# Context and key operands laid in longer rows, key blocks cut at 320 and 296 columns

## Chip, cores and metric

The kernel runs on one NeuronCore of a Trainium2 chip (trn2). The metric is the device time of one execution in microseconds, lower is better; the time of a kernel is the median of its runs.

## What is computed

Four cross-attention layers follow each other on a stream `x` of shape (8, 512, 512). All four attend to the same context `ctx` of shape (8, 77, 1024). Layers 0 and 2 are of one kind ("A"), layers 1 and 3 of another ("B"). Cut to what matters:

```python
def kind_A(x, ctx, mask_A, mask_B, Wq, Wk, Wv, Wo, bo, tok_A, tok_B):   # 16 heads of 64
    q, k, v = heads(x @ Wq), heads(ctx @ Wk), heads(ctx @ Wv)
    logits = einsum('bhqd,bhkd->bhqk', q, k) * 64 ** -0.5
    bias = zeros((512, 77))
    bias[:, tok_A] = -20 * (1 - mask_A)[:, None]
    bias[:, tok_B] = -20 * (1 - mask_B)[:, None]
    out = einsum('bhqk,bhkd->bhqd', softmax(logits + bias), v)
    return merge(out) @ Wo + bo + x

def kind_B(x, ctx, wq, wk, wv, wo, norm_w):                             # 16 heads of 32, 4 key heads
    q = heads(rmsnorm(x, norm_w) @ wq)
    k, v = heads(ctx @ wk), heads(ctx @ wv)
    out = softmax_over_context(q, k, v, scale=32 ** -0.5)
    return x + merge(out) @ wo
```

Everything is float32.

## The kernel before

Every product of two float32 matrices is made of three TensorE passes: an operand is split in a part rounded to `fp32r` ("hi") and the rest ("lo"), and the passes are hi x hi, hi x lo and lo x hi (`three_passes`, L259 to L263, or the same three written out). Each pass is one MATMUL with a weight load of its own (the stationary operand, up to 128 columns), then up to 512 columns of the moving operand stream past it.

**The context part** (`context_part`, L290 to L597) comes first. `ctx_s` holds the transposed context, hi and lo: for each of 8 chunks `k` of 128 channels a row of 616 values (8 batches x 77 tokens). For each of nine blocks of 256 weight columns (`j`), TensorE makes

- the keys: for two groups `m` of 128 columns and two halves `h` of the 616 context columns (`n = 2m + h`), 8 chunks x 3 passes with the weights stationary and `ctx_s` **moving**, 308 columns each: `keys` at L558, 9 x 4 x 8 x 3 = 864 matmuls;
- the values: for five groups `r` of 128 context columns (the last has 104) 8 chunks x 3 passes with `ctx_s` **stationary** and 256 weight columns moving: `values` at L567, 9 x 5 x 8 x 3 = 1080 matmuls.

ScalarE rounds each result out of its bank (L415, L422), VectorE subtracts for the rest (L464, L470), and the SP queue stores both in DRAM (`k_scr`, `v_scr`). `k_out`, the tile that the keys are stored from, has rows of 616 values.

**The main part** (`whole_block`) walks over 128 units (four layers x eight batches x four groups of heads; unit `u` uses slot `u % 2`). For each unit the SP queue loads keys into `keys_s[:, slot]` (L699), block-diagonal, so that one matmul serves several heads; TensorE makes the scores of four tiles of 128 tokens. For kind A a tile takes 2 x 3 matmuls of 154 columns (`keys[:, c, h]`, L807, L810, L813: `c` is a pair of heads, `h` hi or lo), for kind B it takes 3 matmuls of 308 columns (L824, which is L261 to L263). So 1536 short ones of kind A and 768 of kind B have `keys_s` as moving operand. The short ones are issued one by one between matmuls of 512 columns of the query projection (L847 to L851) or of the values (L889): `beside`, L942, with two of 512 columns after each short one in tiles 0 and 1 of a steady unit. VectorE takes the maximum and subtracts (L1165, L1169), ScalarE exponentiates, POOL multiplies by the reciprocal sums (L1326), TensorE transposes (L869), multiplies by the values (L889), and projects (L261 to L263 on `acc_bank`). The order on each engine is written out by hand in step loops; four groups of PSUM banks with two banks each pass the work on.

**Where the operands lie.** The tensors are placed one behind the other in each partition. In the kernel before, `w_s`, `x_s`, `o_s`, `q_s`, `ctx_s` and `keys_s` begin on a multiple of 128 bytes and the rows of the first four are 2048 bytes or more. A row of `ctx_s` is 616 x 4 = 2464 bytes, which is 19 x 128 + 32, and the second half of a row begins 1232 bytes in, which is 9 x 128 + 80. So the moving operand of the keys begins 0, 32, 64, 96, 0, 32, 64, 96 bytes past a multiple of 128 for `k` = 0 to 7 in the first half and 80, 112, 16, 48, 80, 112, 16, 48 in the second; hi and lo alike. In `keys_s` a slot has 2464 bytes and a kind A block 616: the short operands `(c, h)` = (0,0), (0,1), (1,0), (1,1) begin 0, 104, 80, 56 bytes past a multiple of 128 in slot 0, and 32, 8, 112, 88 in slot 1. Those of kind B, `h` = 0 and 1, begin 0 and 80 past it in slot 0, 32 and 112 in slot 1. `x_front`, `mx`, `sums`, `rinv` and `ms` begin 64 past one. The context part's tensors are given back at once (`early.close()`, L347), so the main part's lie over them: `o_s` to `unused` over `ctx_s`, `q_s` over `kvw_raw`, `prob` over `k_out`, `pT_s` over `v_out`.

Of the kernel before, what the change touches and what calls it, by code (L numbers as in the profile page):

```python
# [36 lines left out]
SC = GH * CTX  # L37
PART = 2048
BLK = 256
HALF = ROWS // 2  # L40
SUPPRESS, EPS = 20.0, 1e-5
VROWS = [min(P, ROWS - P * r) for r in range(-(-ROWS // P))]

# [246 lines left out]
def context_part(nc, ctx, lasting, ctxT, kvw, k_scr, v_scr, k1_scr, v1_scr, x_in, wqA, boA, normB, masks, tokens,  # L290
# [7 lines left out]
    def sb(name, shape, dt):  # L298
        return early.enter_context(nc.sbuf_tensor(name, shape, dt))
# [2 lines left out]
        return ctx.enter_context(nc.semaphore(name))  # L302

    ctx_raw = sb("ctx_raw", [P, KC, ROWS], F32)
    ctx_s = sb("ctx_s", [P, 2, KC, ROWS], F32R)
    w_raw = sb("kvw_raw", [P, 2, PART], F32)
    k_out = sb("k_out", [P, 2, 2, ROWS], F32R)
    v_out = sb("v_out", [P, len(VROWS), 2, BLK], F32R)
# [89 lines left out]
    def scalar(act):  # L398
        def split_weights(slot, j):
            if j:  # L400
                act.wait_ge(w_loaded[slot], 16 * (j + slot))
                if slot == 0:
                    act.wait_ge(k_mm, 4 * j)
                else:
                    act.wait_ge(v_mm, NV * j)
            else:
                act.wait_ge(w_loaded[slot], 16)
            act.activation(w_s[:, slot, 0], w_raw[:, slot], ACT.Copy).then_inc(w_hi[slot], 1)

        def drain_keys(n, j):  # L410
            m, h = n // 2, n % 2
            act.wait_ge(k_mm, 4 * j + n + 1)
            if n == 0 and j:
                act.wait_ge(k_stored, keys_stored(j))
            act.activation(k_out[:, m, 0, h * HALF:(h + 1) * HALF], banks[n][:, 0:HALF], ACT.Copy)\  # L415
               .then_inc(k_hi, 1)

        def drain_values(r, j):
            act.wait_ge(v_mm, NV * j + r + 1)
            if r == 0 and j:  # L420
                act.wait_ge(v_stored, vals_stored(j))
            act.activation(v_out[0:VROWS[r], r, 0], banks[4 + r % 4][0:VROWS[r], 0:BLK], ACT.Copy)\  # L422
               .then_inc(v_hi, 1)

        def split_late(n):

            act.wait_ge(late_loaded[n], 16)
            act.activation(late_parts(n)[0], w_raw[:, n % 2], ACT.Copy).then_inc(late_hi, 1)

        for k in range(KC):  # L430
            if k % 2 == 0:
                act.wait_ge(first_loaded[k // 2], 16)
                act.activation(w_s[:, 0, 0, BLK * k:BLK * (k + 2)], w_raw[:, 0, BLK * k:BLK * (k + 2)], ACT.Copy).then_inc(first_hi, 1)
            if k == 0:
                act.wait_ge(chunk_loaded, 16)
            else:
                act.wait_ge(ctx_loaded[k // 2], 16)
            act.activation(ctx_s[:, 0, k], ctx_raw[:, k], ACT.Copy).then_inc(ctx_hi, 1)
        split_weights(1, 0)
        for j in range(NJ):  # L440
            for n in range(4):
                drain_keys(n, j)
            if j + 1 < NJ:
                split_weights(0, j + 1)
            else:
                split_late(1)
                split_late(2)
            for r in range(NV):
                drain_values(r, j)
            if j + 1 < NJ:  # L450
                split_weights(1, j + 1)
            if j + 2 == NJ:
                split_late(0)

    def vector(dve):
# [5 lines left out]
        def drain_keys(n, j):  # L461
            m, h = n // 2, n % 2
            dve.wait_ge(k_hi, 4 * j + n + 1)
            dve.tensor_tensor(k_out[:, m, 1, h * HALF:(h + 1) * HALF], banks[n][:, 0:HALF],  # L464
                              k_out[:, m, 0, h * HALF:(h + 1) * HALF].bitcast(F32), ALU.subtract)\
               .then_inc(k_lo, 1)

        def drain_values(r, j):
# [9 lines left out]
        for k in range(KC):  # L478
            if k % 2 == 0:
                dve.wait_ge(first_hi, k // 2 + 1)  # L480
                dve.tensor_tensor(w_s[:, 0, 1, BLK * k:BLK * (k + 2)], w_raw[:, 0, BLK * k:BLK * (k + 2)],
                                  w_s[:, 0, 0, BLK * k:BLK * (k + 2)].bitcast(F32), ALU.subtract).then_inc(first_lo, 1)
            dve.wait_ge(ctx_hi, k + 1)
            dve.tensor_tensor(ctx_s[:, 1, k], ctx_raw[:, k], ctx_s[:, 0, k].bitcast(F32), ALU.subtract)\
               .then_inc(ctx_lo, 1)
        split_weights(1, 0)
        links = [0]
# [69 lines left out]
    def tensor(pe):  # L557
        def keys(n, k):  # L558
            m, h = n // 2, n % 2
            mm = three_passes(pe, banks[n][:, 0:HALF],  # L560
                              [w_s[:, 0, s, BLK * k + m * P:BLK * k + m * P + P] for s in range(2)],
                              [ctx_s[:, s, k, h * HALF:(h + 1) * HALF] for s in range(2)],
                              k == 0, k == KC - 1)
            if k == KC - 1:
                mm.then_inc(k_mm, 1)

        def values(r, j):  # L567
            if NV * j + r >= 4:
                pe.wait_ge(v_lo, NV * j + (1 if r == 4 else 0))
            for k in range(KC):  # L570
                mm = three_passes(pe, banks[4 + r % 4][0:VROWS[r], 0:BLK],
                                  [ctx_s[:, s, k, r * P:r * P + VROWS[r]] for s in range(2)],
                                  [w_s[:, 1, s, BLK * k:BLK * (k + 1)] for s in range(2)],
                                  k == 0, k == KC - 1)
            mm.then_inc(v_mm, 1)

        for k in range(KC):
            if k % 2 == 0:
                pe.wait_ge(first_lo, k // 2 + 1)
            pe.wait_ge(ctx_lo, k + 1)  # L580
            for n in range(4):
                keys(n, k)
        for j in range(NJ):
            if j:
                pe.wait_ge(w_lo[0], j)
                pe.wait_ge(k_lo, 4 * j)
                for n in range(4):
                    for k in range(KC):
                        keys(n, k)
            pe.wait_ge(w_lo[1], j + 1)  # L590
            for r in range(NV):
                values(r, j)
# [7 lines left out]
def whole_block(nc, lasting, context_args, x_in, stream, k_scr, v_scr, k1_scr, v1_scr, wqA, woA, wqB, woB):  # L600

    with ExitStack() as ctx:
# [7 lines left out]


        vals_s = sb("vals_s", [P, 2, 4, 2, P], F32R)
        keys_s = sb("keys_s", [P, 2, 2 * SC], F32R)
        x_front = sb("x_front", [P, RING, TOK], F32)
        mx = sb("mx", [P, 2, 4 * GH], F32)
        sums = sb("sums", [P, 2, 4 * GH], F32)
        rinv = sb("rinv", [P, 2, 4 * GH], F32)
        ms = sb("ms", [P, 2, TILES], F32)
        rstd = sb("rstd", [P, 2, TILES], F32)

        o_s = sb("o_s", [P, 2, 8, TOK], F32R)
        xsq = sb("xsq", [P, TOK], F32)
        x_power = sb("x_power", [P, TOK], F32)
        rest = sb("rest", [P, TILES, P], F32)
        sb("unused", [P, 128], F32)

        q_s = sb("q_s", [P, 2, 2, 2, TOK], F32R)
        prob = sb("prob", [P, 2, TILES, SC], F32)
# [166 lines left out]
        def _(pe):  # L795
            def scores(u, t):
                slot, out, tok = u % 2, s_bank[t % 2], slice(t * P, t * P + P)
                if kind(u).name == "A":
                    pe.wait_ge(s_biased, plan.biased(u, t))
                    keys = keys_s[:, slot].rearrange("q (c h n) -> q c h n", c=2, h=2)  # L800
                    for c in range(2):
                        if t == 0:
                            pe.wait_ge(q_out, plan.q[("q", u, c)] + 1)
                            if c == 0:
                                pe.wait_ge(keys_loaded[slot], plan.keys_count(u))
                        cols = out[:, 2 * CTX * c:2 * CTX * (c + 1)]
                        pe.matmul(cols, q_s[:, slot, 0, c, tok], keys[:, c, 0], start=False, stop=False,  # L807
                                  skip_group_check=True)
                        yield
                        pe.matmul(cols, q_s[:, slot, 0, c, tok], keys[:, c, 1], start=False, stop=False,  # L810
                                  skip_group_check=True)
                        yield
                        mm = pe.matmul(cols, q_s[:, slot, 1, c, tok], keys[:, c, 0], start=False, stop=c == 1,  # L813
                                       skip_group_check=True)
                        if c == 1:
                            mm.then_inc(s_mm, 1)
                        yield
                else:
                    pe.wait_ge(s_sub, TILES * u + t - 1)
                    if t == 0:  # L820
                        pe.wait_ge(q_out, plan.q[("q", u, 0)] + 1)
                        pe.wait_ge(keys_loaded[slot], plan.keys_count(u))
                    keys = keys_s[:, slot].rearrange("q (h n) -> q h n", h=2)
                    three_passes(pe, out[:, 0:SC], [q_s[:, slot, h, 0, tok] for h in range(2)],  # L824
                                 [keys[:, h] for h in range(2)], True, True).then_inc(s_mm, 1)
                    yield
# [635 lines left out]
```

## Time and profile before

| | us |
|---|---|
| time of the kernel before, median of 3 runs | 2069.18 (2068.88 to 2070.52) |
| the profiled execution | 2069.05 |
| its span, first to last instruction | 2067.3 |
| PE (matmuls) busy | 2027.7, 98% of the span, 11482 matmuls |
| PEld (weight loads) busy | 1762.3, 85% |
| VectorE busy | 1404.0, 68% |
| ScalarE busy | 966.7, 47% |
| POOL busy | 646.3, 31% |

The profile is of one execution. Matmuls are pipelined and their ends are modelled, so that busy time on PE says little of how many more could be done; how long a matmul holds the engine is read from the starts: the distance from one start to the next in a stretch where nothing is waited for. The granted TensorE clock is shown in tenths of full speed (2.4 GHz).

### The profile page before, as it was taken

The numbers are of one execution on the slowest core, as the hardware profiler recorded it, in microseconds if no ns is written. First come the engines' busy times: TensorE is split into PE (matmuls) and PEld (weight loads), VectorE is DVE, ScalarE is ACT, GpSimd is POOL, SyncE is SP. The second block draws the span as 40 slices with busy tenths as digits, with TensorE's granted clock in tenths as the row PEclk, the third lists the DMA queues.
The fourth block names the chain that finished last, engine by engine and source line by source line (L and its number), as shares of the span: only waits on it lengthen the run. The fifth ranks groups of instructions, "written<-read, shape, count | busy, mean of one in ns | idle before, by whom it ended". The sixth has DMA issues, their size and how long they took to land.

```text
span 2067.3 us, 31200 instructions
## 1 busy us (share of the span) xinstructions
PE 2027.7 (98%) x11482; PEld 1762.3 (85%) x11482; DVE 1404.0 (68%) x2424; ACT 966.7 (47%) x1814; POOL 646.3 (31%) x518
## 2 busy tenths in 40 slices
PE   8999999999999998999999999999999989999998
PEld 8999988888888887788888888888888877888887
DVE  4432365775568556788888676557755675888886
ACT  3222263553445344555555454335433553555553
POOL 0000042322232254454443441223212533444441
PEclk9999999999999999999999999999999999999999
DMA  8688832222122222233333332212221232233322
GB/s 232 165 172 195 187 94 62 73 67 74 54 73 70 66 83 71 83 106 97 88 97 95 104 98 64 76 56 68 65 79 51 72 90 68 74 91 92 88 72 84
DMA packets 262537, 191.02 MB, mean 92 GB/s; under 512 B 197522, under 2 KB 199986, under 8 KB 259826
## 3 DMA queue, kind: packets, MB, share of 16 engines
q1 hardware_dynamic: 262386, 189.03, 34.8%
q8 instruction: 92, 1.51, 0.3%
q14 instruction: 59, 0.48, 0.1%
HBM read 132.66 MB, written 56.26 MB: 91 GB/s over the span
## 4 chain that ended last, share of the span: by engine, by line
PE 50%; issue 30%; POOL 11%; DVE 6%; ACT 1%; DMA 1%; SPq 0%; POOLq 0%; DVEq 0%; ACTq 0%
PE acc_bank L889 6%; POOL prob L1326 6%; PE t_bank L869 4%; PE acc_bank L261 4%; PE acc_bank L263 4%; PE acc_bank L262 4%; PE ctx_bank L261 4%; PE ctx_bank L262 4%; PE ctx_bank L263 4%; PE q_bank L847 4%; PE q_bank L849 3%; PE q_bank L851 3%; POOL x_s L1301 3%; PE s_bank L261 2%; POOL rest L1335 2%
## 5 line engine op out<-in xcount | busy, mean ns | idle before, releaser
L1326 POOL TENSOR_TENSOR prob<-prob,rinv 128x1232 f32<-128x1232 f32 x128 | 288.3, 2253 | 1011.4 <-DVE rinv L1207 1011.4
L1065 ACT ACTIVATE q_s<-q_bank 128x512 fp32r<-128x512 f32 x192 | 114.7, 597 | 491.6 <-PE q_bank L851 488.5
L889 PE MATMUL acc_bank<-pT_s,vals_s 128*128 128x512 f32 x1024 | 339.4, 417 | 0.0
L847 PE MATMUL q_bank<-x_s,w_s 128*128 128x512 f32 x768 | 319.9, 417 | 0.0
L849 PE MATMUL q_bank<-x_s,w_s 128*128 128x512 f32 x768 | 313.6, 408 | 0.0
L851 PE MATMUL q_bank<-x_s,w_s 128*128 128x512 f32 x768 | 313.0, 408 | 0.0
L1165 DVE TENSOR_REDUCE mx<-s_bank 128x4 f32<-128x308 f32 x512 | 239.9, 469 | 106.5 <-PE s_bank L813 54.1
L261 PE MATMUL acc_bank<-o_s,w_s 128*128 128x512 f32 x752 | 300.3, 399 | 0.2
L263 PE MATMUL acc_bank<-o_s,w_s 128*128 128x512 f32 x752 | 293.5, 390 | 0.0
L262 PE MATMUL acc_bank<-o_s,w_s 128*128 128x512 f32 x752 | 292.9, 390 | 0.0
L1056 ACT ACTIVATE prob<-prob,rstd 128x308 f32<-128x308 f32 x256 | 141.5, 553 | 265.5 <-DVE prob L1169 255.1
L1169 DVE TENSOR_TENSOR prob<-s_bank,mx 128x308 f32<-128x308 f32 x512 | 244.9, 478 | 26.4
L1192 DVE TENSOR_TENSOR pT_s<-t_bank,pT_s 128x512 fp32r<-128x512 f32 x256 | 175.6, 686 | 79.0 <-ACT pT_s L1079 79.0
L889 PEld LDWEIGHTS acc_bank<-pT_s,vals_s 128*128 128x128 f32 x1024 | 191.8, 190 | 28.3
L1224 DVE SCALAR_TENSOR_TENSOR x_back<-acc_bank,bo,x_back 128x512 f32<-128x512 f32 x64 | 47.8, 747 | 244.9 <-PE acc_bank L263 244.9
L1079 ACT ACTIVATE pT_s<-t_bank 128x512 fp32r<-128x512 f32 (+1 forms) x320 | 183.1, 589 | 35.0 <-PE t_bank L869 34.6
L869 PE MATMUL t_bank<-ident,prob 128*128 128x128 f32 (+1 forms) x1280 | 185.8, 274 | 1.1 <-DVE pT_s L1192 1.1
L1204 DVE TENSOR_REDUCE sums<-prob 128x16 f32<-128x1232 f32 x128 | 182.5, 1426 | 0.0
L869 PEld LDWEIGHTS t_bank<-ident,prob 128*128 128x128 f32 (+1 forms) x1280 | 155.7, 136 | 28.6 <-DVE pT_s L1192 1.6
L263 PEld LDWEIGHTS acc_bank<-o_s,w_s 128*128 128x128 f32 x752 | 141.1, 188 | 30.6
L261 PEld LDWEIGHTS acc_bank<-o_s,w_s 128*128 128x128 f32 x752 | 141.3, 188 | 28.7 <-DVE o_s L1198 1.8
L851 PEld LDWEIGHTS q_bank<-x_s,w_s 128*128 128x128 f32 x768 | 145.6, 190 | 23.2
(107 smaller groups left out, 4095.0 us busy)
## 6 DMA issues: line engine op xcount, KB each, us to landing
stream<-x_back SPq DMA_DIRECT2D x128, 256.0 KB, 2.6
x_front<-stream SPq DMA_DIRECT2D x96, 256.0 KB, 3.3
x_back<-stream SPq DMA_DIRECT2D x96, 256.0 KB, 3.9
kvw_raw<-kvw SPq DMA_DIRECT2D x17, 1024.0 KB, 8.4
k_scr<-k_out SPq DMA_DIRECT2D x36, 308.0 KB, 8.8
keys_s<-k_scr SPq DMA_DIRECT2D x128, 77.0 KB, 2.5
v_scr<-v_out SPq DMA_DIRECT2D x8, 1024.0 KB
vals_s<-v_scr SPq DMA_DIRECT2D x512, 6.5 KB
```

The costliest lines, as they stand in the source:

```text
L261: pe.matmul(out, weights[0], moving[0], start=start, stop=False)
L262: pe.matmul(out, weights[0], moving[1], start=False, stop=False)
L263: return pe.matmul(out, weights[1], moving[0], start=False, stop=stop)
L847: pe.matmul(out, w[0], x_now[0], start=k == 0, stop=False)
L849: pe.matmul(out, w[0], x_now[1], start=False, stop=False)
L851: mm = pe.matmul(out, w[1], x_now[0], start=False, stop=k == XC - 1)
L869: mm = pe.transpose(t_bank[(3 * u + n) % 2][0:rows, t * P:t * P + P], p, ident[:, :])
L889: mm = pe.matmul(out, w, pT_s[:, part], start=i == mine[0] and part == 2 * n and w is v[0], stop=i == mine[-1] and w is terms[-1][0] and p ...
L1079: act.activation(pT_s[0:rows, 2 * n], t_bank[(3 * u + n) % 2][0:rows, :], ACT.Copy).then_inc(t_hi, 1)
L1165: dve.tensor_reduce(top, scored, AX_X, ALU.max).then_inc(s_max, 1)
L1169: dve.tensor_tensor(prob[:, slot, t].rearrange("q (h n) -> q h n", h=GH), scored, top.unsqueeze(2).broadcast_to([P, GH, CTX]), ALU.subtrac ...
L1326: pool.tensor_tensor(view, view, rinv[:, slot].unsqueeze(2).broadcast_to([P, TILES * GH, CTX]), ALU.mult).then_inc(p_norm, 1)
```

## The change

`ctx_s` gets rows of 640 values (2560 bytes, 20 x 128) of which 616 are used, and the halves of the keys are 320 and 296 columns, so that the second begins 1280 bytes in. In `keys_s` a kind A block gets 160 values (640 bytes) of which 154 are used, a kind B block 320 (1280 bytes) of which 308 are used; a slot is 2560 bytes. So all moving and stationary operands in these two tensors begin on multiples of 128 bytes. `ms` and `rstd` move behind `rest`, and `unused` grows from 128 to 336 values. With that `x_front`, `mx`, `sums`, `rinv` and `ms` begin on multiples of 128 bytes too, `o_s`, `xsq`, `x_power` and `rest` lie 128 bytes higher, and `q_s`, `prob`, `pT_s`, `x_back` and `stage` 1024 bytes higher. `q_s` then begins 512 bytes below `kvw_raw` instead of on it.

The number and order of the instructions on each engine, the SP queue's among them, and what each waits for stay as they were. Forms change: the 864 key matmuls of 308 columns become 432 of 320 and 432 of 296, the 36 pairs of drains (L415, L464) likewise 18 of 320 and 18 of 296, and eight clears of `keys_s` on POOL take 640 instead of 616 values. Rows in DRAM, in `k_out` and in `prob` keep their lengths.

```diff
-HALF = ROWS // 2
+HALF = 320
+HALVES = [slice(0, HALF), slice(HALF, ROWS)]
+ROWS_LAID, SC_LAID, PAIR_LAID = 640, 320, 160
...
-    ctx_s = sb("ctx_s", [P, 2, KC, ROWS], F32R)
+    ctx_s = sb("ctx_s", [P, 2, KC, ROWS_LAID], F32R)
...
-            act.activation(k_out[:, m, 0, h * HALF:(h + 1) * HALF], banks[n][:, 0:HALF], ACT.Copy)\
+            cols = HALVES[h]
+            act.activation(k_out[:, m, 0, cols], banks[n][:, 0:cols.stop - cols.start], ACT.Copy)\
...
-            act.activation(ctx_s[:, 0, k], ctx_raw[:, k], ACT.Copy).then_inc(ctx_hi, 1)
+            act.activation(ctx_s[:, 0, k, 0:ROWS], ctx_raw[:, k], ACT.Copy).then_inc(ctx_hi, 1)
...
             m, h = n // 2, n % 2
-            mm = three_passes(pe, banks[n][:, 0:HALF],
+            cols = HALVES[h]
+            mm = three_passes(pe, banks[n][:, 0:cols.stop - cols.start],
                               [w_s[:, 0, s, BLK * k + m * P:BLK * k + m * P + P] for s in range(2)],
-                              [ctx_s[:, s, k, h * HALF:(h + 1) * HALF] for s in range(2)],
+                              [ctx_s[:, s, k, cols] for s in range(2)],
...
-        keys_s = sb("keys_s", [P, 2, 2 * SC], F32R)
+        keys_s = sb("keys_s", [P, 2, 2 * SC_LAID], F32R)
...
-        ms = sb("ms", [P, 2, TILES], F32)
-        rstd = sb("rstd", [P, 2, TILES], F32)
...
-        sb("unused", [P, 128], F32)
+        ms = sb("ms", [P, 2, TILES], F32)
+        rstd = sb("rstd", [P, 2, TILES], F32)
+        sb("unused", [P, 336], F32)
...
-                    keys = keys_s[:, slot].rearrange("q (c h n) -> q c h n", c=2, h=2)
+                    keys = keys_s[:, slot].rearrange("q (c h n) -> q c h n", c=2, h=2)[:, :, :, 0:PAIR]
...
-                    keys = keys_s[:, slot].rearrange("q (h n) -> q h n", h=2)
+                    keys = keys_s[:, slot].rearrange("q (h n) -> q h n", h=2)[:, :, 0:SC]
```

## Rows read from the trace of the kernel before

**Rows 1.** Page: span, busy time of each engine, granted clock in 40 slices.

```profile
span 2067.3 us, 31200 instructions
...
PE 2027.7 (98%) x11482; PEld 1762.3 (85%) x11482; DVE 1404.0 (68%) x2424; ACT 966.7 (47%) x1814; POOL 646.3 (31%) x518
...
PEclk9999999999999999999999999999999999999999
```

**Rows 2.** Groups by line and form (xcount, busy us, mean ns, idle before).

```profile
L813 PE MATMUL s_bank<-keys_s,q_s 128*128 128x154 f32 x512 | 119.5, 233 | 0.0
...
L263 PE MATMUL ctx_bank<-ctx_s,w_s 128*128 128x308 f32 x288 | 88.2, 306 | 0.0
...
L263 PE MATMUL s_bank<-keys_s,q_s 128*128 128x308 f32 x256 | 78.4, 306 | 0.0
...
L263 PE MATMUL ctx_bank<-w_s,ctx_s 128*128 128x256 f32 x288 | 80.8, 280 | 0.0
...
L263 PE MATMUL ctx_bank<-w_s,ctx_s 128*104 128x256 f32 x72 | 20.2, 281 | 0.0
...
L464 DVE TENSOR_TENSOR k_out<-ctx_bank,k_out 128x308 fp32r<-128x308 f32 x36 | 16.7, 476 | 55.7 <-ACT k_out L415 55.7
...
L1364 POOL MEMSET keys_s<- 128x616 f32 x6 | 3.7, 614 | 34.9 <-PE s_bank L813 29.4 <-PE s_bank L263 5.5
```

**Rows 3.** Timeline of PE, a block of context keys (start us, us, engine, line).

```profile
92.20 0.30 PE L261 MATMUL ctx_bank<-ctx_s,w_s 128*128 128x308 f32 x1
...
92.63 0.30 PE L261 MATMUL ctx_bank<-ctx_s,w_s 128*128 128x308 f32 x1
...
94.77 0.30 PE L261 MATMUL ctx_bank<-ctx_s,w_s 128*128 128x308 f32 x1
...
95.18 0.31 PE L261 MATMUL ctx_bank<-ctx_s,w_s 128*128 128x308 f32 x1
...
95.61 0.30 PE L261 MATMUL ctx_bank<-ctx_s,w_s 128*128 128x308 f32 x1
...
99.01 0.31 PE L261 MATMUL ctx_bank<-ctx_s,w_s 128*128 128x308 f32 x1
```

**Rows 4.** Timeline of PE, a projection of 512 columns.

```profile
670.15 0.39 PE L261 MATMUL acc_bank<-o_s,w_s 128*128 128x512 f32 x1
...
672.87 0.39 PE L261 MATMUL acc_bank<-o_s,w_s 128*128 128x512 f32 x1
```

**Rows 5.** Timeline of PE, first values block after those keys.

```profile
105.81 0.28 PE L261 MATMUL ctx_bank<-w_s,ctx_s 128*128 128x256 f32 x1
...
106.17 0.28 PE L261 MATMUL ctx_bank<-w_s,ctx_s 128*128 128x256 f32 x1
...
108.65 0.28 PE L261 MATMUL ctx_bank<-w_s,ctx_s 128*128 128x256 f32 x1
```

**Rows 6.** Timeline of PE, score tiles of units 28 and 29, kind A.

```profile
716.11 0.23 PE L807 MATMUL s_bank<-keys_s,q_s 128*128 128x154 f32 x1
...
717.83 0.23 PE L807 MATMUL s_bank<-keys_s,q_s 128*128 128x154 f32 x1
...
719.57 0.23 PE L807 MATMUL s_bank<-keys_s,q_s 128*128 128x154 f32 x1
...
727.52 0.23 PE L807 MATMUL s_bank<-keys_s,q_s 128*128 128x154 f32 x1
...
729.23 0.23 PE L807 MATMUL s_bank<-keys_s,q_s 128*128 128x154 f32 x1
...
730.94 0.23 PE L807 MATMUL s_bank<-keys_s,q_s 128*128 128x154 f32 x1
```

**Rows 7.** Timeline of PE, transposes, four to a row.

```profile
1015.14 0.60 PE L869 MATMUL t_bank<-ident,prob 128*128 128x128 f32 x4
1015.58 0.60 PE L935 MATMUL q_bank<-ident,x_power 128*128 128x128 f32 x4
```

**Rows 8.** List of waits, a PE row: who waited for whom, total us, times, longest.

```profile
PE s_bank L261 <- DVE prob L1169: 21.9, 24, 3.7
```

More of the change, by code:

```diff
@@ L463, in drain_keys @@
             dve.wait_ge(k_hi, 4 * j + n + 1)
-            dve.tensor_tensor(k_out[:, m, 1, h * HALF:(h + 1) * HALF], banks[n][:, 0:HALF],
-                              k_out[:, m, 0, h * HALF:(h + 1) * HALF].bitcast(F32), ALU.subtract)\
+            cols = HALVES[h]
+            dve.tensor_tensor(k_out[:, m, 1, cols], banks[n][:, 0:cols.stop - cols.start],
+                              k_out[:, m, 0, cols].bitcast(F32), ALU.subtract)\
                .then_inc(k_lo, 1)
@@ L483, in vector @@
             dve.wait_ge(ctx_hi, k + 1)
-            dve.tensor_tensor(ctx_s[:, 1, k], ctx_raw[:, k], ctx_s[:, 0, k].bitcast(F32), ALU.subtract)\
+            dve.tensor_tensor(ctx_s[:, 1, k, 0:ROWS], ctx_raw[:, k], ctx_s[:, 0, k, 0:ROWS].bitcast(F32), ALU.subtract)\
                .then_inc(ctx_lo, 1)
@@ L559, in keys @@
             m, h = n // 2, n % 2
-            mm = three_passes(pe, banks[n][:, 0:HALF],
+            cols = HALVES[h]
+            mm = three_passes(pe, banks[n][:, 0:cols.stop - cols.start],
                               [w_s[:, 0, s, BLK * k + m * P:BLK * k + m * P + P] for s in range(2)],
-                              [ctx_s[:, s, k, h * HALF:(h + 1) * HALF] for s in range(2)],
+                              [ctx_s[:, s, k, cols] for s in range(2)],
                               k == 0, k == KC - 1)
```

## Prediction, made before the changed kernel was run

> **What bounds the kernel.** I read the page first: PE is busy for 2027.7 of 2067.3 us at a granted clock of nine tenths or more in all 40 slices, while VectorE has 68%, ScalarE 47% and POOL 31% [rows 1]. So the time is the sum over TensorE's matmuls of how long each holds the engine, plus some waits, of which the largest that PE itself shows in the scores is 21.9 us in 24 places behind VectorE's subtraction [rows 8]. The change can move the time only by what a matmul costs. I therefore went to the groups by form for the counts, and then to the timeline of PE for distances between starts, because the mean ns of a group has a modelled end in it. At 2.4 GHz a column takes 1/2.4 = 0.4167 ns; what a start-to-start distance has above that I call the excess.
>
> - Keys of the context, 308 moving columns: 48 matmuls from 92.20 to 99.01 us, 6.81 / 48 = 141.9 ns; streaming is 308 / 2.4 = 128.3 ns, excess 13.6 ns [rows 3].
> - A projection, 512 moving columns: 12 matmuls from 670.15 to 672.87, 2.72 / 12 = 226.7 ns; streaming 213.3, excess 13.4 ns [rows 4].
> - Values of the context, 256 moving columns: 24 matmuls from 105.81 to 108.65, 118.3 ns; streaming 106.7, excess 11.6 ns [rows 5].
>
> This is the heart of the matter: the projection's operands (`o_s` and `w_s`) begin on multiples of 128 bytes in the kernel before, those of the keys for the most part do not, and the excess is the same within 0.2 ns. If a start off such a multiple cost anything, the keys would have to show it.
>
> **The change, part by part.** Counts: 864 key matmuls (3 x 288), 1080 value matmuls (3 x 288 + 3 x 72), 768 scores of kind B (3 x 256), 1536 of kind A (3 x 512) [rows 2]; 4248 of 11482 in all. Some begin on a multiple of 128 bytes already: two of the 16 chunks of the keys (108 matmuls), and of kind B's those in slot 0 with `h` = 0 (two passes of three of 384, so 256). That leaves 864 - 108 + 768 - 256 = 1268 of 308 columns that change.
>
> *The split 320/296.* The columns are the same in number. Between 308 and 512 columns the distance grows by (226.7 - 141.9) / 204 = 0.416 ns a column [rows 3, 4], so 320 costs about 5.0 ns more (146.9) and 296 5.0 ns less (136.9): 432 x 5.0 - 432 x 5.0 = 0. Bounds: the line through 256 and 512 columns, (226.7 - 118.3) / 256 = 0.423 a column, puts 308 at 140.3, so 141.9 could hold 1.6 ns of some rounding that 320 and 296 would lose: 864 x 1.6 = 1.4 us of gain; or they could keep it and each pay as much again: +1.4 us. I take 0, since the straight line is what the nearest rows give.
>
> *Alignment of the moving operand, keys.* The block is a trial by itself, because the eight chunks start at all offsets. One chunk is three matmuls. Chunk 0 (offset 0, aligned) takes 92.63 - 92.20 = 0.43 us; chunk 6 (offset 64) takes 95.18 - 94.77 = 0.41 us; the eight of the first half take 3.41 / 8 = 0.426, and the eight of the second half, none aligned, 3.40 / 8 = 0.425 [rows 3]. The aligned one is no cheaper. Upper end: all become like chunk 0, (0.430 - 0.4256) / 3 = +1.5 ns, x 864 = +1.3 us. Lower end: all become like the cheapest chunk, (0.410 - 0.4256) / 3 = -5.2 ns, x 864 = -4.5 us. I take 0: the cheapest is an unaligned one, and its rows are rounded to 0.01 us.
>
> *Scores of kind B.* The same form and width, and the same mean, 306 ns, as the keys [rows 2]; so the same price: 0, between 768 x 1.5 = +1.2 and 768 x -5.2 = -4.0 us.
>
> *Scores of kind A.* A pair `c` of a steady tile is three short matmuls and six of 512. In unit 28 (slot 0) the pair c = 0 takes 717.83 - 716.11 = 1.72 us, c = 1 takes 719.57 - 717.83 = 1.74; in unit 29 (slot 1) both take 1.71 [rows 6]. Slot 1 has no operand on a multiple of 128 and is the quickest. Six long ones are 6 x 0.2267 = 1.36 us, so a short one holds the engine for (1.71 - 1.36) / 3 = 117 ns to 127 ns though its 154 columns stream in 64 ns. Next to it stands the transpose: 128 columns (53 ns), yet one every (1015.58 - 1015.14) / 4 = 110 ns [rows 7]. Both are paced by the 128-column weight load, which hides any saving in the streaming. I take 0. Lower end: the 384 short ones of slot 0, c = 1 fall by the (1.74 - 1.71) / 3 = 10 ns to the others' level, -3.8 us; upper end: slot 1 rises to slot 0's c = 0, 768 x 3.3 ns = +2.5 us.
>
> *Stationary operand, values.* The first chunk (offset 0) takes 0.36 us, the next seven (108.65 - 106.17) / 7 = 0.354 [rows 5]. Aligned is not cheaper. All like the first: (0.36 - 0.355) / 3 = +1.7 ns, x 1080 = +1.8 us; below, the same distance, -1.8 us. I take 0.
>
> *The rest.* The drain of 308 columns takes VectorE 476 ns [rows 2]; in proportion 320 and 296 are 19 ns more and less, under a PE that waits for neither. POOL's clear of `keys_s` at 614 ns grows by at most 24/616 of that, 24 ns in each of eight, on an engine that is idle for 69% of the span. Its cover is large: a step of the main part is many us long. The move of `x_front` and of the small tiles concerns ScalarE, VectorE and POOL, which have 32 to 69% to spare. DMA issues keep number, size and order; no wait is added. Taken at nothing.
>
> **Sum.** 0 + 0 + 0 + 0 + 0 = 0 against the profiled execution's own 2069.05 us (span 2067.3 and 1.75 around it); the median of the runs is 2069.18, 0.13 above, and I predict **2069.2 us**. With every upper end at once it would be +1.4 + 1.3 + 1.2 + 2.5 + 1.8 = +8.2 us, with every lower end -1.4 - 4.5 - 4.0 - 3.8 - 1.8 = -15.5 us. The ends are independent and those below rest on the cheapest single readings, so the likeliest case has as its own range within 0.2% (4.1 us, about what a measurement of this kernel can tell from no change): 2065.1 to 2073.3.
>
> The Trainium skill (TensorE: Matmul & The Clock Gate, "Back-to-back issue gap") gives the gap of an isolated matmul as N / 2.4 + 2.5 ns, which would be 130.8 for 308 columns where the trace has 141.9. If aligned starts brought those 1268 matmuls down to it, that would be 11.1 ns x 1268 = 14.1 us of gain, an estimate of 2055 us. The trace speaks against it: the aligned 512 columns would be 215.8 ns by the page and take 226.7 [rows 4].
>
> **Rivals.**
>
> 1. *Off-multiple starts are the excess* (faster). 13.3 ns is just what 32 columns cost (32 / 2.4), and 32 columns are 128 bytes: each start between two multiples could cost one more piece of that size. Then the 1268 matmuls save 13.3 ns each, 16.9 us, and the result is 2052.3; the short ones stay at the weight load's pace. For it: the size of the excess. Against it: the aligned projection has the same excess, and chunk 0 takes no less than its neighbours [rows 3, 4]. Chance 0.05.
> 2. *A smaller saving of the same sort* (faster). The lower ends are partly real: steps of a chunk do differ by up to 0.02 us [rows 3]. If aligned operands all come out as the cheapest ones, 2069.2 - 15.5 = 2053.7; about half of it is 2061. Against it: in no stretch is the cheapest the aligned one. Chance 0.08.
> 3. *Aligned streams meet* (slower). The weight load of the next matmul and the moving operand of this one are read at the same time. With both on multiples of 128 they would begin in the same place each time and could hold each other up. Place: the 1268 matmuls of 308 columns. Price: chunk 0 is 0.43 where the mean is 0.4256; with the rounding of the rows against me it is 0.44, (0.44 - 0.4256) / 3 = 4.8 ns, x 1268 = 6.1 us, so 2075.3. It decides from 4.1 us / 1268 = 3.2 ns each. For it: the first chunk of keys and of values is each time the dearer [rows 3, 5]. Against it: the all-aligned projection has no more excess than the rest. Chance 0.07.
> 4. *The change does not do what it says*: streaming could be charged by whole pieces of 32 columns, so that 308, 320 and 296 all cost the same; or the transposes, whose `prob` rows of 1232 bytes stay unaligned, could be what matters. Either gives no difference in time and counts with the forecast.
>
> **How the numbers follow.** Within 0.2%: 0.80. Faster: 0.05 + 0.08 = 0.13. Slower: 0.07. For the range I take the 0.80 and reach a little into rivals 2 and 3, to 2062 (some 7 us of the 15.5) and 2075; outside lie rival 1, the larger half of rival 2 and the tail of rival 3, some 0.13.
>
> **What would show it.** Right: in the keys block pairs of halves still take 6.8 us for 48 matmuls, with 0.441 us for a chunk of 320 and 0.411 for one of 296; a kind A pair stays at 1.71 to 1.74 us; the transposes stay at 110 ns; PE stays busy for 98%. Wrong toward faster: 48 key matmuls in 6.2 us, or kind A pairs below 1.70. Wrong toward slower: the chunk of 320 above 0.45, or the eight value chunks of a group above 2.88 us. The forecast as a whole is wrong if the time leaves 2065.1 to 2073.3.

## The result, and the profile after

The changed kernel takes 2081.76 us (median of 4 runs, 2081.33 to 2082.30) against 2069.35 us before (4 runs, 2068.88 to 2070.52). The ratio is 1.0059, with a 95% interval from 1.0046 to 1.0073: it is slower by 12.4 us, where no change had been forecast and the range ended at 2075. The profiled execution took 2082.3 us with a span of 2080.5, so 13.2 us more than the span before.

The page first, the lines that answer to [rows 1]:

```profile
span 2080.5 us, 31200 instructions
...
PE 2039.4 (98%) x11482; PEld 1762.5 (85%) x11482; DVE 1404.3 (67%) x2424; ACT 966.7 (46%) x1814; POOL 645.3 (31%) x518
...
PEclk9999999999999999999999999999999999999999
```

The other engines are busy within 1 us of what they were; PE is busy for 11.7 us more at the same number of matmuls, and the granted clock stays at nine tenths or more in every slice. So the time is in what matmuls cost, as the prediction had it, and the question is which. The groups by line and form (count, busy us, mean ns, idle before) answer; the changed kernel's lines have numbers two to five higher, so that `three_passes` is L263 to L265:

```profile
L263 PE MATMUL acc_bank<-o_s,w_s 128*128 128x512 f32 x752 | 303.0, 403 | 2.5 <-DVE o_s L1203 2.5
L265 PE MATMUL acc_bank<-o_s,w_s 128*128 128x512 f32 x752 | 297.1, 395 | 0.0
L264 PE MATMUL acc_bank<-o_s,w_s 128*128 128x512 f32 x752 | 296.6, 394 | 0.0
...
L263 PE MATMUL ctx_bank<-w_s,ctx_s 128*128 128x256 f32 x288 | 81.5, 283 | 0.0
...
L265 PE MATMUL s_bank<-keys_s,q_s 128*128 128x308 f32 x256 | 78.2, 306 | 0.0
...
L265 PE MATMUL ctx_bank<-ctx_s,w_s 128*128 128x320 f32 x144 | 45.0, 313 | 0.0
...
L265 PE MATMUL ctx_bank<-ctx_s,w_s 128*128 128x296 f32 x144 | 43.4, 302 | 0.0
```

Compared with [rows 2] the scores of kind B are unchanged (306 ns), and the keys' two forms, 313 and 302 ns, lie about their old 306. What has grown is a group that the change does not name: the projection of the attention's result, `acc_bank<-o_s,w_s`. In the kernel before its three lines are

```profile
L261 PE MATMUL acc_bank<-o_s,w_s 128*128 128x512 f32 x752 | 300.3, 399 | 0.2
L263 PE MATMUL acc_bank<-o_s,w_s 128*128 128x512 f32 x752 | 293.5, 390 | 0.0
L262 PE MATMUL acc_bank<-o_s,w_s 128*128 128x512 f32 x752 | 292.9, 390 | 0.0
```

against 303.0, 297.1 and 296.6 us here: 10.0 us more. The timeline of PE shows how. This is a stretch of a projection in the changed kernel (start us, us), the counterpart of [rows 4]:

```profile
675.70 0.39 PE L263 MATMUL acc_bank<-o_s,w_s 128*128 128x512 f32 x1
675.93 0.40 PE L264 MATMUL acc_bank<-o_s,w_s 128*128 128x512 f32 x1
676.16 0.39 PE L265 MATMUL acc_bank<-o_s,w_s 128*128 128x512 f32 x1
676.39 0.40 PE L263 MATMUL acc_bank<-o_s,w_s 128*128 128x512 f32 x1
676.63 0.39 PE L264 MATMUL acc_bank<-o_s,w_s 128*128 128x512 f32 x1
...
678.50 0.39 PE L263 MATMUL acc_bank<-o_s,w_s 128*128 128x512 f32 x1
```

Twelve matmuls from 675.70 to 678.50 us take 2.80 us, 233.3 ns each, where the kernel before had 226.7. The steps are no longer equal either. At the full resolution of the trace, a group of 96 projection matmuls has its starts 226, 227, 227 ns apart in the kernel before, from the seventh matmul to the last; here they come 229, 238, 229, 237 ns apart, just as regularly. The operands have the same form, the same tensors, the same order; `o_s` lies 128 bytes higher.

The other stretches, the keys block, the values block behind it, and the score tiles of units 28 and 29, against [rows 3, 5, 6]:

```profile
93.59 0.31 PE L263 MATMUL ctx_bank<-ctx_s,w_s 128*128 128x320 f32 x1
...
97.11 0.30 PE L263 MATMUL ctx_bank<-ctx_s,w_s 128*128 128x296 f32 x1
...
100.38 0.31 PE L263 MATMUL ctx_bank<-ctx_s,w_s 128*128 128x320 f32 x1
```

```profile
107.16 0.28 PE L263 MATMUL ctx_bank<-w_s,ctx_s 128*128 128x256 f32 x1
...
107.51 0.28 PE L263 MATMUL ctx_bank<-w_s,ctx_s 128*128 128x256 f32 x1
...
110.03 0.28 PE L263 MATMUL ctx_bank<-w_s,ctx_s 128*128 128x256 f32 x1
```

```profile
722.30 0.23 PE L812 MATMUL s_bank<-keys_s,q_s 128*128 128x154 f32 x1
...
724.02 0.23 PE L812 MATMUL s_bank<-keys_s,q_s 128*128 128x154 f32 x1
...
725.75 0.23 PE L812 MATMUL s_bank<-keys_s,q_s 128*128 128x154 f32 x1
...
733.72 0.23 PE L812 MATMUL s_bank<-keys_s,q_s 128*128 128x154 f32 x1
...
735.44 0.23 PE L812 MATMUL s_bank<-keys_s,q_s 128*128 128x154 f32 x1
...
737.17 0.23 PE L812 MATMUL s_bank<-keys_s,q_s 128*128 128x154 f32 x1
```

Keys: 24 of 320 columns take 3.52 us, 146.7 ns each, and 24 of 296 take 3.27, 136.3; together 6.79 us for 48 against 6.81. Values: 24 take 2.87 us, 119.6 ns each, against 118.3. Kind A: unit 28 has 1.72 and 1.73 us for a pair, as before within 0.01; unit 29 has 1.72 and 1.73 where it had 1.71 twice.

To see the whole, I took the distance from each matmul's start to the next in both traces (all 11482 are in both, in the same order) and summed the differences by kind:

| | us |
|---|---|
| projection, kind A (1536 matmuls) | +8.9 |
| projection, kind B (720) | +1.8 |
| values of the context (1080) | +1.1 |
| keys of the context (864) | +0.6 |
| queries (2304), +1.5 in kind A and -0.6 in kind B | +0.9 |
| values of the main part, scores, transposes, the other 50 | -0.1 |
| sum | +13.2 |

The projection has 10.7 of the 13.2 us. How far such sums can be trusted shows in the fourteen traces of this case: the queries of kind B come out between -2.4 and +0.3 us and the values of the main part between -1.7 and 0.0 in runs that leave the places of their own operands alone, and the first pass of the keys between -0.2 and +1.1. The projection stays within 0.2 us of the kernel before in every run at 226.7 ns but run 11, which has -0.3.

The idle 2.5 us ahead of L263 behind VectorE's `o_s` are new too, but run 1 below has the same 2.5 and not the loss.

### The profile page after: what moved, and what is told of

Read it like the earlier page. It is cut to its first block, busy times and chain, and to the rows that moved or that the text cites. A ratio compares the mean times of both kernels' runs of the same rounds, so it can differ in the third digit from the quotient of the medians.

```text
span 2080.5 us, 31200 instructions
## 1 busy us (share of the span) xinstructions
PE 2039.4 (98%) x11482; PEld 1762.5 (85%) x11482; DVE 1404.3 (67%) x2424; ACT 966.7 (46%) x1814; POOL 645.3 (31%) x518
## 4 chain that ended last, share of the span: by engine, by line
PE 91%; DVE 6%; ACT 1%; issue 0%; SPq 0%; DMA 0%; DVEq 0%; ACTq 0%
PE acc_bank L894 11%; PE acc_bank L263 8%; PE acc_bank L265 8%; PE acc_bank L264 8%; PE q_bank L852 8%; PE q_bank L856 8%; PE q_bank L854 8%; PE t_bank L874 7%; PE ctx_bank L263 4%; PE ctx_bank L264 4%; PE ctx_bank L265 4%; PE s_bank L815 2%; PE s_bank L263 2%; PE s_bank L812 2%; PE s_bank L818 2%; PE s_bank L265 2%
## 5 line engine op out<-in xcount | busy, mean ns | idle before, releaser
L263 PE MATMUL acc_bank<-o_s,w_s 128*128 128x512 f32 x752 | 303.0, 403 | 2.5 <-DVE o_s L1203 2.5
L265 PE MATMUL acc_bank<-o_s,w_s 128*128 128x512 f32 x752 | 297.1, 395 | 0.0
L264 PE MATMUL acc_bank<-o_s,w_s 128*128 128x512 f32 x752 | 296.6, 394 | 0.0
L263 PEld LDWEIGHTS acc_bank<-o_s,w_s 128*128 128x128 f32 x752 | 141.6, 188 | 34.3 <-DVE o_s L1203 4.0
L265 PEld LDWEIGHTS acc_bank<-o_s,w_s 128*128 128x128 f32 x752 | 141.2, 188 | 33.6
L264 PEld LDWEIGHTS acc_bank<-o_s,w_s 128*128 128x128 f32 x752 | 141.5, 188 | 30.5
```

Of the source, the lines that this page charges most:

```text
L263: pe.matmul(out, weights[0], moving[0], start=start, stop=False)
L264: pe.matmul(out, weights[0], moving[1], start=False, stop=False)
L265: return pe.matmul(out, weights[1], moving[0], start=False, stop=stop)
```

## Experiments

Each was timed beside the kernel before, whose median there was 2069.3 to 2069.8 us, and each is a change of places in SBUF; none leaves work out. Runs 1 and 3 also keep the key blocks of 320 and 296 columns. T1: the place of `o_s` decides how far apart the projection's matmuls start. T2: the projection's rhythm is inherited from the changed timing of the stages ahead of it.

### 1. `o_s` back to its place, all else as changed

```diff
-        rinv = sb("rinv", [P, 2, 4 * GH], F32)
         o_s = sb("o_s", [P, 2, 8, TOK], F32R)
...
         rest = sb("rest", [P, TILES, P], F32)
+        rinv = sb("rinv", [P, 2, 4 * GH], F32)
```

> The changed kernel with one thing undone: rinv goes behind rest too, so that o_s, xsq, x_power and rest lie again where they lay before (128 bytes lower); context rows of 640, key blocks of 320/296 and the longer key rows stay. Theory T1 (the address of o_s decides how far apart the projection's matmuls start): projections of kind A return from 229/238 ns alternating to 226.7 ns a matmul, and with 10.7 of the 12.5 us gone the time is 2071 us (2069 to 2073). Theory T2 (the projection's rhythm is inherited from the context part's or the scores' new timing, wherever o_s lies): 2082 us, rhythm 229/238 as in the changed kernel.

2071.11 us (ratio 1.0007, 0.9998 to 1.0016, to the 2069.33 of before). In the projection:

```profile
672.16 0.39 PE L263 MATMUL acc_bank<-o_s,w_s 128*128 128x512 f32 x1
...
674.88 0.39 PE L263 MATMUL acc_bank<-o_s,w_s 128*128 128x512 f32 x1
```

12 in 2.72 us: 226.7 ns. By the distances of the starts the projection is within 0.1 us of the kernel before, where the changed kernel has +10.7. The keys' and context's whole edit is still in, and the loss is gone. T1 holds, T2 falls.

### 2. The kernel before, with `o_s` 128 bytes up and nothing else of the change

```diff
+        sb("gap", [P, 32], F32)
         o_s = sb("o_s", [P, 2, 8, TOK], F32R)
...
-        sb("unused", [P, 128], F32)
+        sb("unused", [P, 96], F32)
```

> The kernel before with one thing done: o_s, xsq, x_power and rest lie 128 bytes higher (a gap of 32 values ahead of o_s, 32 fewer behind rest). T1: projections of kind A start 229/238 ns apart, +8.1 us there and +2.6 us in kind B's, so 2080 us (2077 to 2082). T2: unchanged, 2069.3 us (within 2).

2078.91 us, ratio 1.0045 (1.0032 to 1.0057). The stretch and the group:

```profile
673.77 0.39 PE L261 MATMUL acc_bank<-o_s,w_s 128*128 128x512 f32 x1
...
676.55 0.40 PE L261 MATMUL acc_bank<-o_s,w_s 128*128 128x512 f32 x1
```

```profile
L261 PE MATMUL acc_bank<-o_s,w_s 128*128 128x512 f32 x752 | 302.8, 403 | 0.1
```

12 in 2.78 us, 231.7 ns, and 403 ns in the group's mean as in the changed kernel. The projection sums to +9.6 us over the kernel before, and that is the whole of the loss. So this single displacement makes the kernel slower by 9.6 us, without one operand of the context or the keys being touched.

### 3 and 4. The edits that the change is about, each by itself

Run 3 has `ctx_s` in rows of 640 and the blocks of 320 and 296 columns, run 4 has `keys_s` in rows of 160 and 320 with `rinv`, `ms` and `rstd` moved behind `rest`; in both `o_s` stays where it was.

> The kernel before with the context part's edit alone: rows of 640 in ctx_s, key blocks of 320 and 296 columns; keys_s and the main part's places as before. T1: +1.7 us from the context part (1.1 of it in the value matmuls, 119.7 against 118.6 ns), 2071 us, projections at 226.7 ns. T2 in its first form (the context part's timing sets the rhythm for all that follows): 2082 us.

2070.80 us, ratio 1.0007 (0.9998 to 1.0015): no difference that the runs can tell, though the trace shows where 1.2 us went, into the values of the context:

```profile
L263 PE MATMUL acc_bank<-o_s,w_s 128*128 128x512 f32 x752 | 300.3, 399 | 0.3
...
L263 PE MATMUL ctx_bank<-w_s,ctx_s 128*128 128x256 f32 x288 | 81.5, 283 | 0.0
```

The values group has 81.5 us and 283 ns where a pass had 80.8 to 81.0 us and 280 to 281 ns before ([rows 2] has one of the three), and the sum over the starts is +1.2 us for the values and +0.1 for the keys. The second row is the one to read twice: **laid on multiples of 128 bytes, the stationary operands made the values slower**, not quicker. The three traces with the long context rows have +1.1 to +1.2 us there, the ten others -0.4 to +0.3.

> The kernel before with the keys_s edit alone (blocks of 160 and 320 values); rinv, ms and rstd move behind rest so that o_s and all behind it stay where they were, while x_front, mx and sums move up by 192 bytes. T1: nothing in the projections, 2069 to 2070 us. T2 in its second form (the scores' timing sets the rhythm): 2080 us.

2070.16 us, ratio 1.0006 (0.9997 to 1.0015). The projection is at its old cost:

```profile
L262 PE MATMUL acc_bank<-o_s,w_s 128*128 128x512 f32 x752 | 300.3, 399 | 0.1
```

The starts put +0.5 us on the scores of kind A, +1.5 on the queries between them and -0.6 on those of kind B. The three traces with the long key rows have 2.0 to 2.1 us in kind A's scores and queries together, those in which `keys_s` keeps its place at most 0.8. No gain from aligned keys anywhere.

### 5. Everything 128 bytes up

```diff
+        sb("low_gap", [P, 32], F32)
         self.w_s = sb("w_s", [P, 4, 2, PART], F32R)
```

> The kernel before with every tensor of both parts 128 bytes higher (a gap of 32 values ahead of w_s), so that o_s has the same place in the partition as in the changed kernel but keeps its distance to w_s, from which the stationary operand of the projection is loaded. Theory R (the distance between the two operands that are read together decides): 2069.3 us, projections of kind A at 226.7 ns. Theory S (the place of o_s alone decides, wherever w_s is): 2079 us, projections at 232 ns.

2069.67 us against 2069.83 (ratio 1.0000, 0.9991 to 1.0009).

```profile
671.18 0.39 PE L261 MATMUL acc_bank<-o_s,w_s 128*128 128x512 f32 x1
...
673.90 0.39 PE L261 MATMUL acc_bank<-o_s,w_s 128*128 128x512 f32 x1
```

226.7 ns, with `o_s` at the very place that cost 9.6 us in run 2. The place of `o_s` by itself does nothing; theory S, that this place alone decides, falls. Theory R, that the distance to the other operand decides, holds so far. What counts is where `o_s` lies **in relation to something else that moved too**.

### 6. The neighbours of `o_s`

The gap of 32 values behind `o_s` instead of ahead of it.

> The kernel before with the gap of 32 values behind o_s: xsq, x_power and rest lie 128 bytes higher, o_s as before. Both theories R and S, which say that it is o_s: 2069.3 us, projections at 226.7 ns. Rival: xsq, x_power or rest, which POOL, ScalarE and TensorE read and write, carry the loss of the run with the gap ahead of o_s: 2079 us.

2070.19 us, ratio 1.0003 (0.9994 to 1.0012); the projection:

```profile
670.30 0.39 PE L261 MATMUL acc_bank<-o_s,w_s 128*128 128x512 f32 x1
...
673.02 0.39 PE L261 MATMUL acc_bank<-o_s,w_s 128*128 128x512 f32 x1
```

226.7 ns. `xsq`, `x_power` and `rest` are acquitted.

### 7 to 10. Other distances

Run 2 with gaps of 64, 96, 16 and 8 values: `o_s` and what follows it 256, 384, 64 and 32 bytes up.

> The kernel before with o_s, xsq, x_power and rest 256 bytes higher. If what counts is whether o_s begins an even or an odd number of 128-byte pieces from w_s (before: an even number), the projection is quick again: 226.7 ns and 2069 us. If it counts in 512 bytes (before: 256 past a multiple of 512 from w_s; here: on one, as x_s is), projections take up to 232 ns and the time is up to 2080 us.

> The kernel before with o_s, xsq, x_power and rest 384 bytes higher. By even and odd pieces of 128 bytes it is like the run with 128: 232 ns in kind A's projections, 2079 us. If only the exact place of the changed kernel is bad, 226.7 ns and 2069 us.

> The kernel before with o_s, xsq, x_power and rest 64 bytes higher: the operands of the projection then begin off every multiple of 128 bytes. Theory U (a start off a multiple of 128 costs, which is what the change wants to remove): each of the 2304 projection matmuls takes longer than 226.7 ns, at 5 ns 2081 us. Theory R (what counts is how w_s and o_s lie to each other within 256 bytes): something between the quick and the slow place, 226 to 232 ns, 2069 to 2080 us; it is known for the values of the context that chunks 64 and 96 bytes off took 117 ns where those on a multiple took 118, so 225 to 226 ns and 2066 us are possible as well.

> The same with 32 bytes. Theory U: as with 64 bytes, 2081 us. Theory R: nearer to the place of before than 64 bytes is, 226 to 229 ns, 2067 to 2074 us.

The same twelve matmuls in each, in that order:

```profile
670.12 0.39 PE L261 MATMUL acc_bank<-o_s,w_s 128*128 128x512 f32 x1
...
672.84 0.39 PE L261 MATMUL acc_bank<-o_s,w_s 128*128 128x512 f32 x1
```

```profile
672.94 0.39 PE L261 MATMUL acc_bank<-o_s,w_s 128*128 128x512 f32 x1
...
675.72 0.40 PE L261 MATMUL acc_bank<-o_s,w_s 128*128 128x512 f32 x1
```

```profile
671.30 0.39 PE L261 MATMUL acc_bank<-o_s,w_s 128*128 128x512 f32 x1
...
674.04 0.39 PE L261 MATMUL acc_bank<-o_s,w_s 128*128 128x512 f32 x1
```

```profile
674.58 0.39 PE L261 MATMUL acc_bank<-o_s,w_s 128*128 128x512 f32 x1
...
677.38 0.39 PE L261 MATMUL acc_bank<-o_s,w_s 128*128 128x512 f32 x1
```

From the sizes of `w_s`, `x_s`, `ident`, the four small lasting tensors, and `vals_s` to `rstd`, `w_s` and `o_s` begin 65536 + 32768 + 512 + 2560 + 19712 = 121088 bytes apart in the kernel before, which is 473 x 256. (The 2560 takes the 16 bytes of `mhalf` as 32; no trace holds an address, so the zero of this scale rests on that, while the steps between the runs do not.) Against that:

| `o_s` up by | distance to `w_s`, past a multiple of 256 | 12 matmuls | ns each | time, us | ratio |
|---|---|---|---|---|---|
| 0 | 0 | 2.72 | 226.7 | 2069.3 to 2069.8 | |
| 256 | 0 | 2.72 | 226.7 | 2069.49 | 0.9999 (0.9990 to 1.0008) |
| 64 | 64 | 2.74 | 228.3 | 2071.83 | 1.0011 (1.0002 to 1.0020) |
| 128 | 128 | 2.78 | 231.7 | 2078.91 | 1.0045 (1.0032 to 1.0057) |
| 384 | 128 | 2.78 | 231.7 | 2078.68 | 1.0044 (1.0032 to 1.0057) |
| 128, the changed kernel | 128 | 2.80 | 233.3 | 2081.76 | 1.0059 (1.0046 to 1.0073) |
| 32 | 32 | 2.80 | 233.3 | 2080.96 | 1.0053 (1.0040 to 1.0067) |
| all by 128 (run 5) | 0 | 2.72 | 226.7 | 2069.67 | 1.0000 (0.9991 to 1.0009) |

By the starts, the whole projection is at +3.0 us with 64 bytes, +9.6 with 128, +9.7 with 384 and +11.6 with 32. 256 is as 0 and 384 as 128: as far as these two pairs show it, the cost repeats with 256 bytes. Theory U, that a start off a multiple of 128 costs, falls with the run at 64, which is off such a multiple and quicker than the one at 128, which is on it (expected by U: 2081 us; measured: 2071.83). Two expectations were off: that 32 bytes would lie between 0 and 64 (it is the slowest of all), and that 64 might be quicker than 0. The cost is not a slope. In each run the distances between starts repeat in a short cycle (226, 227, 227 at 0; 226, 229, 232 with 225, 230, 231 between at 64; a cycle of eight between 228 and 241 at 128), as if the matmuls and something as regular fell into step with each other. What that would be, no run shows.

### 11. The same for the queries

`x_s` 64 bytes away from its old distance to `w_s`, `o_s` at 256. All that lies between them moves by 64 bytes too, `vals_s`, `keys_s` and the context part's tensors among it.

> The kernel before with x_s and all that follows it in the lasting part 64 bytes higher, and o_s a further 192 bytes, so that o_s is 256 bytes up in all (known to cost nothing) and x_s is 64 bytes off its old distance to w_s. The 2304 matmuls of the queries have x_s as moving operand. Theory U: 2081 us. Theory R: the queries move by as much as the projection does in the run with o_s 64 bytes up.

2069.50 us, ratio 1.0000 (0.9991 to 1.0008), the projection at 226.7 ns:

```profile
670.87 0.39 PE L261 MATMUL acc_bank<-o_s,w_s 128*128 128x512 f32 x1
...
673.59 0.39 PE L261 MATMUL acc_bank<-o_s,w_s 128*128 128x512 f32 x1
```

Theory U falls a second time: 2304 matmuls with moving operands off every multiple of 128, at no cost. But theory R misses too. It would have had the queries dearer by 1.6 ns each, 3.7 us; by the starts they are +0.4 us. Nearly all queries follow each other in runs of two in kind A, with short matmuls between, and in runs of six in kind B, where a projection group of kind A is 96 long. Even at the old distance of 0, direct neighbours in kind B's queries start 233 ns apart (median of 620), not 227. Whether the short runs are the reason was not tried. `vals_s` and `pT_s`, an odd multiple of 128 bytes apart before, are here 64 past a multiple of 256; by the projection's table their matmuls should have come closer together, and their direct neighbours start 232 ns apart (median of 398) instead of 231.

The run settles something else. The projection is as quick as before although `x_s`, `vals_s`, `keys_s` and all between them lie differently to `o_s`. So none of these is what the place of `o_s` counts against.

### 12. Another pair, with the hope of a gain

`pT_s` (moving) begins 85376 bytes behind `vals_s` (stationary) in the kernel before: 333 x 256 + 128. A gap of 32 values ahead of `pT_s` makes it a whole multiple of 256.

> The kernel before with pT_s, x_back and stage 128 bytes higher. pT_s is the moving operand of the 1024 value matmuls of the main part and vals_s the stationary one; in the kernel before they lie an odd number of 128-byte pieces apart, and where those matmuls follow each other they start 231 ns apart (median of 398). Theory R, carried to this pair: with an even number they start 227 ns apart, up to 1024 x 4.4 ns = 4.5 us less, 2065 us (2064.5 to 2068, since in kind A they alternate with short ones). Rival: the finding holds for the projection alone, whose runs of 96 matmuls have time to fall into a rhythm; then 2069.3 us and 231 ns.

2068.24 us against 2069.53, ratio 0.9994 (0.9985 to 1.0003): the lowest time of all runs, but the interval reaches past 1, so not shown to be faster. The stretch of five value matmuls up to the transposes, before and here, and the projection's group:

```profile
1013.99 1.31 PE L889 MATMUL acc_bank<-pT_s,vals_s 128*128 128x512 f32 x5
```

```profile
1013.87 1.30 PE L890 MATMUL acc_bank<-pT_s,vals_s 128*128 128x512 f32 x5
1015.01 0.60 PE L870 MATMUL t_bank<-ident,prob 128*128 128x128 f32 x4
```

```profile
L261 PE MATMUL acc_bank<-o_s,w_s 128*128 128x512 f32 x752 | 300.0, 399 | 0.2
```

Five of them take 1.14 us (228 ns each) where they took 1.15 (1013.99 to 1015.14 us, [rows 7]), which is no more than the rounding. The evidence is in the median distance of two that follow each other directly: 227 ns, where the kernel before has 231 and the other twelve traces 231 or 232. The sum over the starts, -1.4 us for these matmuls, is no evidence: the changed kernel has -1.6 and run 9 has -1.7, with `pT_s` and `vals_s` at their old distance. The hoped 4.5 us were never there, because only 398 of the 1024 follow each other directly, 384 of them in kind B; in kind A short matmuls stand between them.

## Why the prediction was wrong

**What bounds the kernel**: right. PE at 98%, the time being the sum of what matmuls hold the engine; the 13.2 us are all on PE.

**The step that failed** is *The rest*. It priced the move of tensors behind `keys_s` at nothing and spoke of `x_front` and the small tiles alone, although the change also puts `o_s` 128 bytes higher, and `o_s` is the moving operand of 2304 matmuls that are not among the 4248 counted. The term was 0 and measured +10.7 us in the trace of the changed kernel (runs 1 and 2 show it to be the place of `o_s`: 2071.11 us without the move, 2078.91 with it alone). Behind that lies a step of the argument: I compared each operand's start with a multiple of 128 by itself and found no cost, which was true and remains so (runs 5 and 11; the 3.0 us of run 9 come with a changed distance to `w_s`). I concluded that places do not matter. They do, in relation to each other, and the "all-aligned projection" that I took for the neutral case, with its 226.7 ns, was the best of the distances tried, quick because of where its two operands happened to lie.

**The split 320/296**: right. 146.7 and 136.3 ns against 146.9 and 136.9; nothing in sum.

**Alignment of the keys**: right, in both the context and kind B's scores. The +0.6 us that the keys show in the changed kernel are +1.0 in the first pass over the chunks, while data arrives, and -0.4 in the 768 matmuls behind it; all three traces with the long rows have these -0.4.

**Scores of kind A**: taken as 0 with +2.5 as the upper end. Unit 29's pairs went from 1.71 to 1.72 and 1.73 us, toward the level of unit 28's, which is what the upper end was made of; run 4 measures +0.5 us on the scores and +1.5 on the queries between them, 2.0 in kind A.

**Stationary operand, values**: taken as 0 with +1.8 as the upper end; it measured +1.1 to +1.2. Reading the first chunk as the model for all would have been right in sign and near in size: aligned was the dearer place here.

**Rivals.** Rivals 1 and 2 (faster) had nothing in them. Rival 3 (aligned streams meet) had the right kind of cause, the two operand streams of consecutive matmuls, and the right sign, but the wrong place (the 308-column matmuls, which pay nothing) and the wrong condition: it isn't being aligned, for both of the projection's operands are on multiples of 128 at 227 ns and at 232. Its argument against itself, that the aligned projection showed no excess, was a single distance taken for a rule. Rival 4 counted with no difference and was not it; its whole pieces of 32 columns are ruled out by 146.7 and 136.3 ns against 141.9.

The changed kernel and run 2 have the same distance between `o_s` and `w_s`, yet kind A's projections sum to +8.9 us in one and +7.8 in the other, with cycles of 229/238 and of eight steps. So the distance does not fix the cycle wholly; what picks it is open.

## What to carry to other kernels

A tensor's place is part of the kernel: an edit that shifts what lies behind it is an edit of every matmul that reads the shifted tensors. When an edit changes a size in SBUF, list all that moves, and run it once with the rest pinned in place by padding; here that separates 9.6 to 10.7 us of side effect from some 2 us of effect (run 1: +1.8 us, not clear of noise; +2.3 by its starts). And look at the single steps, not only at their mean: here 226, 227, 227 turned into 229, 238 with the same matmuls in the same order, which pointed at how they meet and not at more work.

## What the runs showed of the hardware

- With matmuls of 512 `fp32r` columns, a weight load of 128 columns each, in groups of 96, the distance between starts depended on how far apart the moving and the stationary tensor begin: 226.7 ns with 0 past a multiple of 256 bytes, 228.3 with 64, 231.7 or (in the changed kernel) 233.3 with 128, 233.3 with 32. Moving all tensors together changed nothing. That `w_s` is the partner is inferred: it is the projection's other operand, runs 6, 11 and 12 rule out the rest of the main part's tensors but `q_s` and `prob`, and in run 12 the same even distance between `pT_s` and `vals_s` took 231 to 227 ns. No run moved `w_s` by itself. The Trainium skill (SBUF — State Buffer, "A bandwidth-pool intuition that's wrong (but worth ruling out)") gives TensorE a second, independent read port for weight loads. These runs do not show that the two streams share a port, but their places were not independent in effect.
- It isn't a rule for every form. With 256 columns moving from `w_s` and `ctx_s` stationary, all starts at whole multiples of 256 from each other gave 119.6 ns, the mixed starts of the kernel before 118.3. With 308 columns, eight different offsets in a row gave nearly the price of the aligned rows (-0.4 us over 768 matmuls, about 0.5 ns each). The queries, in runs of two and six, moved by +0.4 us with 64 bytes, within what traces differ by.
- A start off a multiple of 128 bytes, or even of 64, showed no cost by itself: the run with `x_s` 64 bytes off (2069.50 us) and those with `ctx_s` and `keys_s` in their old rows (2069.3 to 2069.8) are no slower than run 1 (2071.11), in which these two are aligned.
